# Attention and FFN block on one core: distance tables in eight pieces of 256 columns, the first head's table in two loads, the FFN weights' scale and one V batch placed earlier

## What is computed

```python
H, K, HD = 16, 21, 8
d = rel[None, None, :] - offsets[:, :, None]          # rel = -(s-1) .. s-1
table = (amplitudes[:, :, None] * exp(-abs(sharpness)[:, :, None] * d * d)).sum(axis=1)   # one row per head
k, v, q = split(layernorm(x) @ w_in, 3)
scores = einsum('bhqd,bhkd->bhqk', q, k) / sqrt(HD) + table[:, idx[None, :] - idx[:, None] + (s - 1)]
attn = softmax(scores) @ v
a, g = split(attn @ w_gate + b_gate, 2)
x = x + a * sigmoid(g)
w_fp8, w_scale = quant_fp8(weight)                     # scale = min(448 / max|weight|, 448)
x_fp8, x_scale = quant_fp8(layernorm(x))
x = x + (x_fp8 @ w_fp8.T) * (x_scale * w_scale) + bias
```

## Time and profile before

| | |
|---|---|
| median of 3 runs | 605.04 us |
| the profiled execution | 605.02 us, its span 603.2 us |
| busy: PE | 571.2 us (95%) |
| busy: ACT | 550.9 us (91%) |
| busy: DVE | 547.5 us (91%) |
| busy: POOL | 73.1 us (12%) |
| mean granted TensorE clock | 0.97 |

### The profile page before, as it was taken

The page is one execution under the profiler, slowest core; times in us unless marked ns, Lnnn a source line. Parts: engine busy times, 40 slices in busy tenths (PEclk is TensorE's granted clock), DMA queues, the critical chain, the costliest instruction groups (busy, mean ns, idle before and its releaser), DMA issues.

```text
span 603.2 us, 12655 instructions
## 1 busy us (share of the span) xinstructions
PE 571.2 (95%) x4070; PEld 159.4 (26%) x4070; DVE 547.5 (91%) x666; ACT 550.9 (91%) x610; POOL 73.1 (12%) x91
## 2 busy tenths in 40 slices
PE   9986999999999999999999999999999999999745
PEld 4633122222222222222222222222222222226532
DVE  5964899999999999999999999999999999994975
ACT  5864899999999999999999999999999999993665
POOL 5272200000100010001000100010001000101820
PEclk9998799999999999999999999999999999999958
DMA  7335404032513241325132413241324132410004
GB/s 187 139 102 175 136 18 131 24 113 60 134 35 113 60 132 37 111 62 135 34 110 63 135 34 109 64 132 37 109 64 130 39 108 66 108 32 1 2 0 139
DMA packets 29007, 51.61 MB, mean 86 GB/s; under 512 B 9173, under 2 KB 20478, under 8 KB 28030
## 3 DMA queue, kind: packets, MB, share of 16 engines
q1 hardware_dynamic: 27102, 50.88, 30.0%
q10 hardware_dynamic: 1888, 0.53, 0.4%
HBM read 42.13 MB, written 9.01 MB: 85 GB/s over the span
## 4 chain that ended last, share of the span: by engine, by line
ACT 42%; issue 38%; PE 5%; DVE 4%; ACTq 1%; DVEq 0%; SPq 0%
ACT pbuf L1108 17%; ACT split L1108 17%; ACT split L1116 3%; ACT pbuf L1116 2%; PE ps L1274 2%; PE ps L1024 1%; PE ps L999 1%; DVE split L1478 1%; ACTq L1107 1%; PE ps L1283 1%; DVE stats L1463 1%; DVE amax L1485 0%; DVE pbuf L1454 0%; DVE pbuf L1058 0%; ACT kb L1414 0%
## 5 line engine op out<-in xcount | busy, mean ns | idle before, releaser
L1058 DVE TENSOR_TENSOR split<-ps,t 128x1024 f32<-128x1024 f32 x192 | 233.4, 1224 | 10.8 <-PE ps L999 5.4
L1058 DVE TENSOR_TENSOR pbuf<-ps,t 128x1024 f32<-128x1024 f32 x192 | 231.1, 1220 | 7.9 <-PE ps L999 3.3
L1108 ACT ACTIVATE pbuf<-pbuf 128x1024 f32<-128x1024 f32 x192 | 204.5, 1259 | 6.2 <-DVE pbuf L1058 6.0
L1108 ACT ACTIVATE split<-split 128x1024 f32<-128x1024 f32 x192 | 202.4, 1267 | 1.8 <-DVE split L1058 1.8
L999 PE MATMUL ps<-qb,kb 33*128 33x512 f16 x1024 | 182.8, 391 | 6.6 <-ACT pbuf L1116 2.4
L1024 PE MATMUL ps<-pbuf,vst 128*32 128x512 f32 x1024 | 137.7, 610 | 0.0
L1024 PE MATMUL ps<-split,vst 128*32 128x512 f32 x1024 | 136.0, 604 | 1.0 <-ACT split L1116 1.0
L999 PEld LDWEIGHTS ps<-qb,kb 33*128 33x128 f16 x1024 | 48.5, 93 | 292.0 <-DVE pbuf L1058 110.6
L1008 PE MATMUL ps<-t64s,ident 128*64 128x512 f16 x512 | 80.5, 395 | 0.0
L1116 ACT ACTIVATE split<-ps 128x1024 f32<-128x1024 f32 x64 | 78.6, 1229 | 0.0
L1116 ACT ACTIVATE pbuf<-ps 128x1024 f32<-128x1024 f32 x64 | 78.0, 1220 | 0.0
(11 more groups left out here) (150 smaller groups left out, 300.7 us busy)
## 6 DMA issues: line engine op xcount, KB each, us to landing
t<-g_scratch SPq DMA_DIRECT2D x16, 960.0 KB
kb<-k_scratch SPq DMA_DIRECT2D x120, 64.0 KB
t64s<-gh_scratch SPq DMA_DIRECT2D x16, 248.0 KB
t64s<-gl_scratch SPq DMA_DIRECT2D x16, 248.0 KB
qb<-q_scratch SPq DMA_DIRECT2D x60, 64.0 KB
x_sb<-in_L_attn_x SPq DMA_DIRECT2D x4, 512.0 KB, 7.7
q_scratch<-split SPq DMA_DIRECT2D x8, 256.0 KB, 2.7
k_scratch<-split SPq DMA_DIRECT2D x8, 256.0 KB, 2.7
```

Of the source, the lines that this page charges most:

```text
L1058: eng.tensor_tensor(slot(g, b), banks(unit(k), 2), t128[p][:, t * P:t * P + S], ALU.add).then_inc(z_ready, 1)
L1108: eng.activation(buf, buf, ACT.Exp).then_inc(p_ready, 1)
```

## The change

Four things are changed, all in the first block but for one wait.

1. The distance table is made as eight pieces of 256 columns instead of four of 512, and only for 16 heads: bank 6 now has, in partitions 32c to 32c+31, piece 2c for 16 heads and piece 2c+1 for 16 heads. Each piece is its own matmul; the window into `sel`, which got 16 columns of zeros ahead, puts the amplitudes to the upper or the lower 16 rows, and both are summed. `gv`, `gvh`, `gvl` have 256 columns instead of 512, and the three stores have the shape 8x16x256 instead of 4x32x512.
2. Head 0's `t128` is loaded in two parts: 1280 columns, then the two `t64` halves, then the last 640 columns on a semaphore of their own, `rest_in`, for which DVE waits at group 3.
3. The scale of the FFN weights moves from the end of the block into and behind `bias_vectors`.
4. `v_of(2)` moves ahead of `norms`, `first_queries` move behind `first_keys(2)`, and the banks are given out anew.

```diff
-        sel = sb("sel", [PP, PG, 32], F32)
+        sel = sb("sel", [PP, PG, 48], F32)
...
+        FIRST_T = 3
+        FIRST_W = S + (FIRST_T - 1) * P
+
+        def load_first_bias(eng):
+
+            eng.dma_start(t128[0][:, 0:FIRST_W], slice_of(g_dram, 0, P, FIRST_W)).then_inc(head_in[0], 16)
+            load_bias_parts(eng, 0, 0, head_in[0])
+            v = g_dram[0, :]
+            eng.dma_start(t128[0][:, FIRST_W:T128W],
+                          bass.AP(tensor=v.tensor, offset=v.offset + FIRST_W, ap=[[1, P], [1, T128W - FIRST_W]]))\
+               .then_inc(rest_in, 16)
...
                 for src, dst in ((gv, g_dram), (gvh, gh_dram), (gvl, gl_dram)):
-                    eng.dma_start(dst.rearrange("h (c n) -> c h n", n=HALF), src[:, :]).then_inc(g_out, 16)
+                    eng.dma_start(dst[0:H].rearrange("h (c n) -> c h n", n=PIECE), src[:, :]).then_inc(g_out, 16)
                 eng.wait_ge(g_out, 16 * 3)
-                load_bias(eng, 0, 0, head_in[0])
-                load_bias_parts(eng, 0, 0, head_in[0])
+                load_first_bias(eng)
...
                                 (turn, 2), (gaussian, 2), (q_high, 2), (k_high, 2), (turn, 3), (k_square, 2),
-                                (bias_copies, 0), (q_high, 3), (k_high, 3), (k_square, 3), (first_keys, 0),
-                                (first_keys, 1), (first_queries, 0), (first_queries, 1), (first_keys, 2),
-                                (first_queries, 2), (first_queries, 3), (v_copy, 2), (v_copy, 3), (weights, 0)):
+                                (bias_copies, 0), (q_high, 3), (weights, 0), (k_high, 3), (k_square, 3), (v_copy, 2),
+                                (first_keys, 0), (first_keys, 1), (first_keys, 2), (first_queries, 0),
+                                (first_queries, 1), (first_queries, 2), (first_queries, 3), (v_copy, 3)):
...
+                scales(eng, 7, 0)
                 eng.wait_ge(gh_ready, 2)
...
-                scales(eng, 1, 0)
                 eng.wait_ge(flag_ready, 1)
...
                     for g in range(PG):
                         eng.wait_ge(exp_ready, g + 1)
-                        for c in range(4):
-                            last = eng.matmul(ps[32 * c:32 * c + 32, 6, :], sel[:, g, :],
-                                              gauss[g][:, c * HALF:(c + 1) * HALF],
-                                              start=(g == 0), stop=(g == PG - 1))
+                        if g == PG - 1:
+                            turn_maximum(eng, NLN + 1, 7, 0)
+                        for a in range(2):
+                            for c in range(4):
+                                k = 2 * c + a
+                                last = eng.matmul(ps[32 * c:32 * c + 32, 6, 0:PIECE], sel[:, g, H - H * a:2 * H + H - H * a],
+                                                  gauss[g][:, k * PIECE:(k + 1) * PIECE],
+                                                  start=(g == 0 and a == 0), stop=(g == PG - 1 and a == 1))
                     last.then_inc(gsum_ready, 1)
+                    spread_scale(eng, 7, 0)
...
+                    if b == 0 and g == FIRST_T:
+                        eng.wait_ge(rest_in, 16)
```

More of the change, by code:

```diff
@@ L38 @@
 HALF = 512
+PIECE = 256
 PAIRS = H * KB
@@ L231, in attention_block @@
         vst_in = sem("vst_in")
+        rest_in = sem("rest_in")
         groups_done = sem("groups_done")
@@ L685, in first_queries @@
                         for i in range(2):
-                            last = eng.matmul(ps[64 * c:64 * c + 64, 6 + b % 2, :], pick[:, i, :], split[:, i, t],
+                            last = eng.matmul(query_ps(b)[64 * c:64 * c + 64, :], pick[:, i, :], split[:, i, t],
                                               start=(i == 0), stop=(i == 1))
@@ L754, in _ @@
                 eng.transpose(ps[0:1, 0, 256:259], bndr[0:3, :], ident[0:3, 0:3]).then_inc(bndt_ready, 1)
[L755 to L756 removed]
+                first_queries(0)
                 first_keys(3)
[L758 to L760 removed]
+                for b in range(1, B):
+                    first_queries(b)
                 v_of(3)
[L762 to L764 removed]
                 eng.wait_ge(flag_ready, 1)
```

70 lines of the change are left out of this document (34 added, 36 removed).

## The result

The changed kernel takes 601.43 us (median of four runs, 601.25 to 601.74); the kernel before, run beside it, 605.04 (604.74 to 605.09). The ratio is 0.9946, 95% interval 0.9934 to 0.9958. It was faster by 3.6 us, and the forecast was 601.5. The profiled execution took 601.45, its span is 599.6 (before 603.2). In a second session the same kernel gave 601.01 (600.59 to 601.5) against 604.66, ratio 0.9931 (0.9911 to 0.9952). One of that session's 17 executions of the kernel before took 1772.86 us, three times as long as the others, and is not counted in the ratio.

What follows compares the result with a forecast made beforehand. The loop runs at ACT's pace, so only its start could move: block end 3.2 us earlier (51.4 instead of 54.58) plus 0.3 us from the clock, gain 3.5, from 605.02 to 601.5 us; range 600.3 to 603.6.

Steps and rivals of the forecast that it cites:

- What bounds the kernel: Loop: goes at ACT's pace, 128 groups of 3.74 us, unchanged; only the loop's start can move.
- Part 1: Block's end: moving the scale removes the 2.16 us tail; around the table, k comes about 0.67 us late.
- with about 0.15 us for the small matmul: Behind the table: after the spreading matmul at 35.72, q of the fourth batch starts at 35.85, 0.55 us late.
- Part 2: Table in eight pieces: 48 matmuls at most 0.066 us each, 0.2 us more per third; halved evictions give 0.4 back.
- The instruction bound: Rival at the table: each smaller matmul costs as much as one of 512 columns, 2.6 us more, 604.1; chance 0.07.
- Part 3: Table's stores and loads: load issued at 42 to 43.5, landed at 47 to 48.5; by itself no gain, only cover.
- at 97 GB/s: Table's stores: half the bytes on the same four engines need 2.7 us instead of 5.4, on eight half of that.
- Part 4: V's third batch fills PE's 1.31 us wait ahead of `norms`; V's fourth starts at 48.45, its copy ends at 51.4.
- Sum, the handover: Between block's end and loop: 2.02 us to PE's start kept; block ends at 51.4, loop starts at 53.4.
- Sum, the clock: Loop's start: clock low again about as long, 2.3 us of cost before; only 0.3 us gained on first scores.
- The short walk: Rival in the first block: hand-overs or table matmuls cost 1 to 2 us unseen, 602.4 to 603.8; chance 0.14.
- The rival that the table lands late: PE's first score waits for `head_in[0]` once stores take over 11.3 us; slower, 607 at 17 us; chance 0.04.

Runs made afterwards that it cites:

- scale_late: Changed kernel with the scale's work and the turn of `wffn` back at the first block's end; 603.66 us, ratio 0.9986.
- table_four: Changed kernel with the distance table as four pieces of 512 columns again, stored as 4x32x512; 602.44 us, ratio 0.9962.
- four_stores_first: Changed kernel with four table pieces, and SP storing the fourth batch of q and k before head 0's loads; 602.07 us, ratio 0.9958.
- flag_early: Kernel before, with DVE and PE reading the flag ahead of the scale's work instead of behind it; 603.99 us, ratio 0.9994.
- after_again: The changed kernel itself run once more, nothing changed; 601.01 us, ratio 0.9931.
- keep_clock: Changed kernel with 19 unused matmuls on zeros: 5 behind V's last batch, 3 ahead of the first score, 11 behind first scores; 600.16 us, ratio 0.9928.
- zeros_later: Changed kernel with 16 unused matmuls on zeros behind V's last batch and the first scores, none ahead of the first score; 599.67 us, ratio 0.9912.
- zeros_split: Changed kernel with V's fourth copy cut between ACT and DVE, and zero matmuls (3 behind V, 11 behind first scores); 599.35 us, ratio 0.9929.

## Why the prediction was right

The time was right to 0.1 us, the account was not in all its terms.

- **What bounds the kernel.** Right: the pace is 3.75 before and after (87.47 - 83.72 is 3.75, not 3.74), and 3.50 us of the gain are there at group 3.
- **Part 1.** Right: scale_late shows the tail of 2.16 us come back. The step "with about 0.15 us for the small matmul" was too small: from the spreading matmul to q are 0.31 us. q starts 3.54 us behind the table's start, where the prediction had 35.85 - 32.59 = 3.26.
- **Part 2.** Right: 0.058 us for each row where at most 0.066 was allowed. The instruction bound would have shown 0.1075.
- **Part 3.** The issue of the load was put at 42 to 43.5 and came at 40.36, because the stores took 3.76 us where 9.06 less 2.7 to 4.1, so 5.0 to 6.4, was expected. The step "at 97 GB/s" took the rate of 42 to 44 us for the whole and left 3.7 us as fixed. In the kernel before the stages of 38 to 42 us have 23, 8, 49 and 86 GB/s at a DMA share of 0.17 to 0.23, so that was transfer too, and it shrank with the rest: from SP's last issue to the last landing are 7.1 us before and 1.7 now. The step "this costs nothing and, by itself, brings nothing" was wrong. It put SP's end at 51.56, "just at the new end", and left out what SP does behind its last store, the read of the flag until 52.7 in table_four. And the landing was put 3.3 + 1.5 = 4.8 us behind the load's issue. No row shown with it gives the 1.5, and by the semaphore's records the landing takes 8.5 us in the kernel before (46.39 to 54.85), 7.8 in the changed one (40.36 to 48.17) and 7.3 to 8.9 in the runs here, with other transfers in flight beside it. In table_four it holds the first score until 54.35, in four_stores_first until 53.68. Eight pieces bring 1.0 to 1.4 us of the 3.6, not none. The total didn't suffer: with all four changes made this is cover that the forecast took for granted.
- **Part 4.** Right: PE has no wait ahead of `norms`, the second reduction ends at 44.28 (44.3), V's fourth batch starts at 48.44 (48.45). V's copy ends at 51.55 (51.4). But the table itself began 0.39 us earlier than in the first profile, so the walk from the table to the end was 0.54 too short: 0.28 at the spreading matmul, 0.10 up to the bound, and 0.16 in V's last batch and its copy. The early start is no part of the change: over all profiles, kernels with the old first block among them, the table begins anywhere from 32.17 to 32.67 (32.59, 32.67 and 32.21 for the kernel before, its second profile and flag_early). In these three the warming matmuls go on at 0.43 us each until 7.0, 7.1 and 4.5 us and at 0.21 from then on, as the clock rises later or earlier.
- **Sum, the handover.** The step "to PE's start are 2.02 us ...; I keep them" failed: 1.28. The wait counts from the engine that ends last with its read of the flag, which was DVE before; now ACT ends last, and it has no flag to read. flag_early shows it on the kernel before. Together: 53.4 expected, + 0.15 for the later copy - 0.74 = 52.83.
- **Sum, the clock.** 0.3 us were to be won at the loop's start, and 0.34 were lost: 487.18 against 486.84 from first score to last exp. The step "I expect the clock low again for about as long" had 14 us in mind; it was 10. It fell at 55.4, so the loop's first 2.6 us ran at the full level. That won what was forecast: from first score to first exp 1.79 us instead of 2.01, and 7.87 for two groups instead of 8.12. But the clock rose 12.9 us behind the first score instead of 11.8, and the third group took 6.51 instead of 5.77 (72.50 - 66.73). The step that failed is that the length of the stretch was priced, and not where in the loop it ends. In after_again a stretch of the same 10 us ended 11.5 us behind the first score and cost 0.5 less. So this term moves by at least 0.5 us between two executions of one kernel, and one profile doesn't give it closer.
- The gain is then 3.77 (start) - 0.34 (loop) + 0.10 (rest) = 3.53 us. The start came 0.57 earlier than forecast and the loop was 0.64 longer: that the total hit is luck of two misses of opposite sign.
- **Rivals.** The short walk was a part of it, 0.5 of its 1 to 2 us. The others fell. The clock's price, 2.3 us over three groups, was right for the kernel before: 72.50 - 58.61 = 13.89 against 67.12 - 55.50 = 11.62 in keep_clock. In the changed kernel it is 2.8. The rival that the table lands late came nearer than its 0.04: its limit of 11.3 us for the stores rests on the 4.8 us of landing. With the measured 7.8 it is 53.4 - 7.8 - 37.3 = 8.3 us, under the old 9.06, so at the stores' old speed the loop would have waited for the table, which is what table_four shows.
- **Signs.** Of those named in advance these failed: the clock was low for 10 us instead of 14 and came back later in the loop, and the first score is 0.57 ahead of 53.4. The others came as written.

## What to carry to other kernels

A block ends with the engine whose last step ends last, and the read of a register at a block's end is such a step: put it where the engine waits anyway, and ahead of the last real work. Before you call a transfer hidden, list all that its queue does until the barrier and when its bytes land, against the new end, not the old. And where a loop's start is moved, read the time from first score to last exp as well: here the clock took 1.2 to 3.8 us of it, and what counted was how far into the loop it came back, not how long it was low.

## What the runs showed of the hardware

- A flag read by DVE or PE at a block's end costs 0.55 + 0.23 and 0.49 + 0.17 us in the sequencers' records, by SP 0.47 to 0.82 + 0.19. The handover is 1.25 to 1.29 us without it on the last engine and 2.02 to 2.03 with it, in the twelve profiles in which the loop's start waits neither for SP nor for the tables.
- With matmuls on zeros in PE's idle time, the clock kept its full level over the 1.25 to 1.37 us that were left without work, and the loop became 2.2 to 2.8 us shorter than the changed kernel's. The Trainium skill (TensorE: Matmul & The Clock Gate, section "Why this matters for your kernels") asks, against drops in the middle of a kernel, that PE have no long idle gaps between bursts of matmuls. keep_clock, zeros_later and zeros_split agree; in the changed kernel PE was idle for 2.3 us ahead of the first score and then only partly busy, and the clock fell.
- Stores of the shape 8x16x256 use 47% of the DMA engines, of 4x32x512 27%. The Trainium skill's rule (DMA: Bandwidth & Descriptors, section "Why a DMA increments its semaphore by 16 and not by 1") gives eight and four of sixteen; both rows agree, and so do the 24 and 12 increments of the stores' semaphore.
